# Reordering three stretches of a transformer-layer kernel on eight cores: the last score tiles, the last query store, and the first loads

## The chip, the cores and the metric

The kernel runs on the eight NeuronCores of one Trainium2 chip. Every core runs the same program on its own part of the data, and no core waits for another. The metric is device time in microseconds of the slowest of the eight cores, from the launch to its end.

A core has a matrix engine (TensorE, PE in the rows), a vector engine (DVE), a scalar engine (ACT), GpSimd (POOL) and SyncE (SP). SP and POOL issue the DMA transfers: SP through the hardware queue q1, POOL through the software queue q0. Both feed the same 16 DMA engines. Each of the five engines runs its instructions strictly in the order in which they were written; semaphores alone hold one engine for another.

## The reference

A sandwich layer on x of shape (4, 4096, 1024):

```
x = x + layernorm(attention(layernorm(x)))       # one head of width 1024
x = x + layernorm(ffn(layernorm(x)))             # 1024 -> 4096 -> 1024
attention: q, k, v = split(x W_qkv^T); softmax(q k^T / 32) v W_out^T
ffn: (gelu(x w1 + b1) w2 + b2) * (sum of the two top router weights, renormalised)
```

The reshape in the reference makes each batch row attend over all 4096 of its tokens. A core takes 2048 query tokens and needs the keys of all 4096 tokens of that batch row (its own 2048, tensor `xo`, and the other half's, `xr`).

## The kernel before, in words

The work is folded so that the projections of keys and values vanish. With A = Wq^T Wk / 32 (`am`, built from `wqb` and `wkb`) the scores are q' xn^T, where xn is the normalised input and q' = xn A. With B = Wv^T Wo^T (`bm`) the output of the attention is (P xn) B. All matrix operands are bf16, all sums f32. PSUM has eight banks of 512 columns, used as four pairs.

The stages, in the order in which TensorE runs them, are:

1. **A**: 64 matmuls for the first 512 columns of `am` in eight banks (outer loop over the eight weight chunks c, inner over the eight row tiles i), then 64 for the second half. Between the row tiles 4 to 7 of the second half stand the TensorE transposes of the first four x tiles (`transpose_x`, L316), each of which needs its tile normalised (`stats_x`, `apply_x`; `norm_next` does the statistics of one unit of tiles and applies those of the unit before, `norm_apply` applies only). The weights of chunks 0 and 1 come through SP in f32 into `stage` and are cast by DVE (L225, L227); chunks 2 to 7 come through POOL, cast on the way.
2. **q'**: four groups of 64 matmuls (`project_q`), with the transposes of the other own tiles in between. ACT moves each result to `qst`; SP stores each group's 1 MB to DRAM scratch `qs`.
3. **B**: 128 matmuls (`form_b`). Meanwhile DVE normalises the 16 tiles of `xr`, and SP transposes each by DMA into the key tensor `xnT` (DT, L111). These 16 transposes are in SP's queue in the order of the tiles.
4. **Attention**, 16 query tiles: `scores(i, c)` for c = 0 to 3 (16 matmuls each, 1024 keys; PSUM pair c modulo 2), reduced by DVE (L507) and exponentiated by ACT (L513); `softmax_tail` and `rescale` on DVE; `transpose_p`, a DMA transpose of the 1 MB probabilities by SP; `context(i)` (64 matmuls, pair 2); `copy_u` and `transpose_u` (a 256 KB DMA transpose); `out_proj(i)` (16 matmuls, pair 3); `finish_a` and `finish_b` (the residual and both norms). Tile i+1 is scored ahead of context i. The residual rows `xf` are loaded by POOL (`load_x`), and each of these loads waits for the last q' store, `t_qs[15]`.
5. **FFN**, four groups of 512 tokens: `ffn1` (256 matmuls with `w1b`, gelu on ACT), router, `ffn2` (256 matmuls with `w2b`), `finish_y`. `w1b` (8 MB) lies over `xnT`, so that its eight loads wait for the scores of the last query tile; `w2b` lies over `xn` and waits for the last context. Six ffn1 blocks of the first group stand between `out_proj(13)` and `context(15)`. `load_x2T` is a 1 MB DMA transpose that brings the first group's tokens.

What a wait on a DMA means here: SP and POOL hold a ring of 16 and 24 semaphores, and each DMA also waits for the one a whole ring before it.

The two lines whose waits the prediction speaks of:

```
t_xf[i] = DG(xf[i % 3][:, :], xo[...], [t_x2s.get(i - 3), t_xnb.get(i - 3), t_qs[NQT - 1]])
for n, after in enumerate([None] + [t_x2T[0]] * 3 + [t_pT[NQT - 1]] * 4): load_w1(n, after)
```

Of the kernel before, what the change touches and what calls it, by code (L numbers as in the profile page):

```python
# [13 lines left out]
H = 1024  # L14
# [64 lines left out]
def build_program():  # L79
# [54 lines left out]
    stage = [at(f"stage{c}", H + 512, F32, R1 + (48 + 6 * c) * KB)  # L134
             for c in range(2)]
# [75 lines left out]
    t_mh = V(lambda e: e.memset(mhalf[:, :], -0.5))  # L211

# [7 lines left out]
    for c in range(2):  # L220
        row = slice(c * 128, (c + 1) * 128)
        f, b = stage[c], c * H
        k = DS(f[:, H:H + 512], wk[row, 0:512])
        q = DS(f[:, 0:H], wq[row, :])
        t_k[0].append(V(lambda e, f=f, b=b: e.tensor_copy(  # L225
            wkb[:, b:b + 512], f[:, H:H + 512]), [k]))
        t_q.append([V(lambda e, f=f, b=b, h=h: e.tensor_copy(  # L227
            wqb[:, b + h:b + h + 512], f[:, h:h + 512]), [q])
            for h in (0, 512)])
    t_id = DS(ident[:, :], idb[:, :])  # L230
    t_b1 = DS(b1f[:, :], b1r[:, :])
    for c in range(2, HC):
        row = slice(c * 128, (c + 1) * 128)
        q = DG(wqb[:, c * H:(c + 1) * H], wq[row, :])
        t_q.append([q, q])
        t_k[0].append(DG(wkb[:, c * H:c * H + 512], wk[row, 0:512]))
# [3 lines left out]
    for t in range(NQT):  # L240
        fetch_x(t)
# [101 lines left out]
    for c in range(HC):  # L343
        for i in range(HC):
            tok = am_part(i, 0, c, i, [t_q[c][i // 4], t_k[0][c]])
            if c == HC - 1:
                am_out(i, 0, i, tok)
    norm_next()
    norm_next()
    for c in range(HC):  # L350
        for i in range(4):
            aft = [t_k[1][c]] if i == 0 else []
            if c == 0:
                aft.append(free[i])
            tok = am_part(i, 1, c, i, aft)
            if c == HC - 1:
                am_out(i, 1, i, tok)
    for i in range(4, HC):
        b = i if i < 6 else i - 6
        for c in range(HC):  # L360
            tok = am_part(i, 1, c, b, [free[b]] if c == 0 else ())
        if i == 4:
            norm_next()
            transpose_x(0)
            am_out(i, 1, b, tok)
        elif i == 5:
            norm_next()
            norm_apply()
            am_out(i, 1, b, tok)
            transpose_x(1)  # L370
        elif i == 6:
            am_out(i, 1, b, tok)
            transpose_x(2)
            transpose_x(3)
            norm_next()
        else:
            am_out(i, 1, b, tok)
# [49 lines left out]

    t_bm = []
# [15 lines left out]
    norm_at = {0: (0, 1, 2, 6), 1: (0, 3, 6), 3: (1, 3, 5, 7)}  # L444
    for g in range(NQG):
        toks = []
        for j in range(HC):
            for k in norm_at.get(g, ()):
                if k == j:
                    norm_next()  # L450
            if g == 2 and j == 0:
                norm_apply()
            project_q(g, j, toks)
            for k, at_j in enumerate((1, 3, 5, 6) if g == 0
                                     else (0, 2, 4, 6)):
                if g < 3 and j == at_j:
                    transpose_x(4 * (g + 1) + k)
        d = DS(qs[4 * g:4 * g + 4].rearrange("k p f -> p k f"),
               qst[g % 3][:, :].rearrange("p (k f) -> p k f", k=4), toks)
        for k in range(4):  # L460
            t_qs[4 * g + k] = d
# [9 lines left out]
    t_bmm = Q.now("tensor")  # L471

# [14 lines left out]
    def scores(i, c):  # L487
        p = i % 2
        pr = c % 2
# [3 lines left out]
        if i == 0 and c < 2:  # L493
            aft += [free[2 * pr], free[2 * pr + 1]]
        else:
            aft.append(pair_free[pr])
        for j in range(HC):
# [16 lines left out]
            [mx, t_bmm, t_cf.get(i - 2), t_pT.get(i - 2)])  # L514

# [163 lines left out]
    for i in range(NQT - 1):  # L679
        last = i == NQT - 2  # L680
# [3 lines left out]
        if last:  # L684
            load_x2T(0)
# [3 lines left out]
        if i >= 1 and not last:  # L689
            out_proj(i - 1)  # L690
            finish_a(i - 1)
        scores(i + 1, 3)
        if i + 2 < NQT:
            load_q(i + 2)
        if i >= 1 and not last:
            finish_b(i - 1)
        if i + 2 < NQT:
            load_x(i + 2)
# [40 lines left out]
    def router(g):  # L739
# [18 lines left out]
        a = A(lambda e: e.activation(rex[:, :], rl[:, :], AF.Exp), [a])  # L758
# [221 lines left out]
```

How the kernel before makes its waits and increments, by code:

```python
            def body(e, items=self.items[eng]):  # L65
                seen = {}
                for after, fn, name, inc in items:
                    for s, v in after:
                        if v > seen.get(s, 0):
                            e.wait_ge(sems[s], v)
                            seen[s] = v
                    ins = fn(e)
                    if name is not None:
                        ins.then_inc(sems[name], inc)
```

## Time and profile before

| | us |
|---|---|
| median of three runs of the kernel | 1112.17 (1111.88 and 1136.29 the others) |
| the profiled execution, its own time | 1113.1 |
| its span on the slowest core (core 7) | 1111.6 |
| spans of the eight cores | 1099.0 to 1111.6 |
| TensorE busy in the span | 1069.6 (96%) |
| matmuls | 5120 |

The profile is of one execution. The span runs from the first instruction to the last on one core; the execution's time has 1.5 us more around it. TensorE is busy nearly throughout, so only what leaves it idle, or at the lower of its two clock levels, can be taken away without removing work. The idle is in a few places, listed by the waits of TensorE.

### The profile page before, as it was taken

To read this page: it belongs to the slowest core of one execution; us is meant where nothing else is said; L and a number is where in the kernel's file an instruction comes from. 1 tells how busy PE (TensorE), PEld (TensorE's weight loads), DVE (VectorE), ACT (ScalarE), POOL (GpSimd) and SP (SyncE) were. 2 spreads that over 40 slices of the span, in tenths; PEclk is the share of its full clock that TensorE was granted. 3 is DMA by queue.
4 is the path that set the end of the run, shared out by engine and by line. 5 is a ranking of instruction groups with operands and counts; after the bars stand their busy time and mean duration, and the time that the engine had idled before them with its cause. 6 is when DMAs were issued, how large, how long until landed. Compare 5 with 4: busy or idle time off the path is not lost.

```text
span 1111.6 us, 13934 instructions; the slowest of 8 cores (1099.0 to 1111.6 us)
## 1 busy us (share of the span) xinstructions
PE 1069.6 (96%) x5120; PEld 487.0 (44%) x5120; DVE 347.7 (31%) x715; ACT 313.3 (28%) x511; POOL 95.8 (9%) x167
## 2 busy tenths in 40 slices
PE   5899969999999999999999989999999999999996
PEld 2454424444444444444444434444444444444443
DVE  0663713433333333433333232124003300330033
ACT  0564412332322223332223213302430143013300
POOL 7130000000000000000000141001000000000000
PEclk9999989999999999999999999999999999999998
DMA  9999974134444443234447999993201230121012
GB/s 151 165 181 204 182 135 86 51 92 90 100 104 105 105 94 82 78 79 103 86 105 137 161 138 195 165 194 110 68 1 42 79 69 1 40 79 34 1 39 75
DMA packets 154834, 111.32 MB, mean 100 GB/s; under 512 B 119696, under 2 KB 129680, under 8 KB 154768
## 3 DMA queue, kind: packets, MB, share of 16 engines
q0 software_dynamic: 30544, 62.15, 28.5%
q1 hardware_dynamic: 124224, 48.29, 21.3%
q8 instruction: 41, 0.67, 0.2%
q14 instruction: 25, 0.20, 0.1%
HBM read 88.69 MB, written 25.17 MB: 102 GB/s over the span
## 4 chain that ended last, share of the span: by engine, by line
PE 81%; DMA 9%; DVE 3%; SPq 2%; issue 2%; POOL 1%; ACT 1%; another core or an unknown queue 0%; DVEq 0%; POOLq 0%; ACTq 0%
PE pAll L115 81%; DMA xn<-xr 4%; DMA xn<-xo 2%; DMA pT<-pb 2%; SPq L111 2%; DVE st L274 1%; DVE st L276 1%; POOL wkb L109 1%; DVE xn L291 0%; DVE pb L536 0%; ACT pb L513 0%; DVE nmx L507 0%; POOL wqb L109 0%; DMA xnT<-xn 0%; DVE yt L823 0%
## 5 line engine op out<-in xcount | busy, mean ns | idle before, releaser
L115 PE MATMUL pAll<-xnT,qt 128*128 128x512 bf16 x1024 | 228.0, 381 | 11.4 <-DMA xnT<-xn 8.7
L115 PE MATMUL pAll<-xn,pT 128*128 128x512 bf16 x1024 | 223.6, 379 | 3.0 <-DMA pT<-pb 3.0
L115 PE MATMUL pAll<-x2T,w1b 128*128 128x512 bf16 x1024 | 222.8, 379 | 0.2 <-DVE yt L823 0.2
L115 PEld LDWEIGHTS pAll<-xnT,qt 128*128 128x128 bf16 x1024 | 100.5, 98 | 134.6 <-issue 15.6
L115 PEld LDWEIGHTS pAll<-xn,pT 128*128 128x128 bf16 x1024 | 100.1, 98 | 124.0 <-issue 3.5
L115 PEld LDWEIGHTS pAll<-x2T,w1b 128*128 128x128 bf16 x1024 | 99.7, 98 | 120.4 <-issue 1.5
L507 DVE TENSOR_REDUCE nmx<-pAll 128x1 f32<-128x1024 f32 x64 | 78.1, 1222 | 204.3 <-PE pAll L115 204.3
L513 ACT ACTIVATE pb<-pAll,nmx 128x1024 bf16<-128x1024 f32 x64 | 71.3, 1114 | 184.8 <-DVE nmx L507 184.8
L115 PE MATMUL pAll<-w2b,h1b 128*128 128x512 bf16 x512 | 115.0, 383 | 2.0 <-DMA w2b<-w 2.0
L115 PE MATMUL pAll<-w2b,h1a 128*128 128x512 bf16 x512 | 113.1, 379 | 0.0
L115 PEld LDWEIGHTS pAll<-w2b,h1b 128*128 128x128 bf16 x512 | 50.5, 99 | 63.9 <-issue 4.7
L852 ACT ACTIVATE x2r<-x2r,nm 128x1024 f32<-128x1024 f32 x15 | 17.2, 1148 | 215.1 <-DVE nm L850 215.1
L115 PEld LDWEIGHTS pAll<-w2b,h1a 128*128 128x128 bf16 x512 | 50.1, 98 | 60.4
L823 DVE TENSOR_TENSOR yt<-pAll,b2b 128x1024 f32<-128x1024 f32 (+1 forms) x17 | 19.7, 1161 | 174.0 <-PE pAll L115 174.0
L735 ACT ACTIVATE h1b<-pAll,b1f 128x512 bf16<-128x512 f32 x64 | 43.2, 687 | 60.0 <-PE pAll L115 59.9
L115 PE MATMUL pAll<-bm,uT 128*128 128x512 bf16 x256 | 57.9, 379 | 0.0
L735 ACT ACTIVATE h1a<-pAll,b1f 128x512 bf16<-128x512 f32 x64 | 42.8, 686 | 53.1 <-PE pAll L115 53.1
L115 PE MATMUL pAll<-xnT,am 128*128 128x512 bf16 x256 | 57.4, 379 | 0.0
L565 ACT CAST ub<-pAll 128x1024 bf16<-128x1024 f32 x16 | 16.2, 1012 | 127.1 <-PE pAll L115 127.1
L115 PE MATMUL pAll<-wkb,wqb 128*128 128x512 bf16 x128 | 32.0, 410 | 13.1 <-DVE wqb L227 12.5
L109 POOL DMA_DIRECT2D x2s<-xf x16 | 8.7, 544 | 383.1 <-DVE xf L626 383.1
L115 PEld LDWEIGHTS pAll<-bm,uT 128*128 128x128 bf16 x256 | 25.0, 98 | 30.2
(87 smaller groups left out, 589.0 us busy)
## 6 DMA issues: line engine op xcount, KB each, us to landing
xf<-xo POOLq DMA_DIRECT2D x16, 512.0 KB, 4.4
x2s<-xf POOLq DMA_DIRECT2D x16, 512.0 KB, 3.2
w1b<-w POOLq DMA_DIRECT2D x8, 1024.0 KB, 18.1
w2b<-w POOLq DMA_DIRECT2D x8, 1024.0 KB, 54.0
x2r<-x2s POOLq DMA_DIRECT2D x16, 512.0 KB, 4.5
y<-yt SPq DMA_DIRECT2D x15, 512.0 KB, 2.7
xn<-xo POOLq DMA_DIRECT2D x16, 256.0 KB, 31.1
xn<-xr POOLq DMA_DIRECT2D x16, 256.0 KB, 53.3
```

What stands on the lines that cost most here:

```text
L109: "gpsimd", lambda e, o=o, i=i: e.dma_start(o, i), after)
L111: "sync", lambda e, o=o, i=i: e.dma_start_transpose(o, i), after)
L115: e.matmul(o, l, m, start=f, stop=s), after, sig)
L274: a = V(lambda e, s=s, xt=xt: e.bn_stats(st[:, s:s + 6], xt[:, 0:512]), [t_x[t]])
L276: b = V(lambda e, s=s, xt=xt: e.bn_stats(st[:, s + 6:s + 12], xt[:, 512:1024]))
L507: mx = V(lambda e: e.tensor_reduce(n, pair[pr], AX, ALU.max, negate=True), [tok, t_cf.get(i - 2)])
L513: lambda e: e.activation(o, pair[pr], AF.Exp, bias=n, accum_out=l),
L565: t_ub[i] = A(lambda e: e.copy(o, pair[2]), [t_ctx[i], t_uT.get(i - 2), t_qs[NQT - 1]])
L735: lambda e: e.activation(o, bank[b], AF.Gelu_apprx_tanh, bias=b1f[:, fc:fc + 1]),
L823: a = V(lambda e, c=c: e.tensor_tensor(o[:, c], pair[pr][:, c], b2b[:, c], ALU.add), [t_f2[(t, (c.stop - 1) // 512)], t_b2] + war)
L852: a = A(lambda e: e.activation(x[:, :], x[:, :], AF.Identity, bias=n_), [t_n, t_x2r[t]])
```

## The change

It has four parts, in the order of the program:

1. The first loads. The f32 staging through SP and DVE goes. POOL loads all eight weight chunks with a cast; x tile 0 is fetched after the fourth of the eight second-half `wkb` chunks in place of after the eighth. One small ACT instruction (`t_tab`) stands ahead of everything. TensorE's order around the first four x tiles changes, and a normalisation unit moves from the first stage into the first q' group.
2. The last q' store stands behind all 16 key transposes in SP's queue. The residual loads, which wait for it, go with it.
3. `scores(1, 2)` and `scores(15, 2)` use PSUM pair 3.
4. The last three query tiles: `scores(14)` and `scores(15)` stand back to back, ahead of the contexts 13, 14 and 15. The output projections 12 and 13 follow their neighbouring contexts. The w1 loads hang on other transfers: 1 to 3 on the transposed probabilities of tile 14, 4 to 7 on `uT` of tile 13.

```diff
-    for c in range(2):
...
-        k = DS(f[:, H:H + 512], wk[row, 0:512])
-        q = DS(f[:, 0:H], wq[row, :])
-        t_k[0].append(V(lambda e, f=f, b=b: e.tensor_copy(
-            wkb[:, b:b + 512], f[:, H:H + 512]), [k]))
...
+    t_tab = A(lambda e: e.activation(rex[:, 0:1], eps[:, 0:1], AF.Ln),
+              [t_eps])
-    for c in range(2, HC):
+    for c in range(HC):
         row = slice(c * 128, (c + 1) * 128)
-        q = DG(wqb[:, c * H:(c + 1) * H], wq[row, :])
-        t_q.append([q, q])
+        t_q.append(DG(wqb[:, c * H:(c + 1) * H], wq[row, :]))
         t_k[0].append(DG(wkb[:, c * H:c * H + 512], wk[row, 0:512]))
     for c in range(HC):
         row = slice(c * 128, (c + 1) * 128)
         t_k[1].append(DG(wkb[:, c * H + 512:(c + 1) * H], wk[row, 512:H]))
-    for t in range(NQT):
+        if c == 3:
+            fetch_x(0)
+    for t in range(1, NQT):
         fetch_x(t)
...
-    norm_next()
     norm_next()
...
+    norm_apply()
     for i in range(4, HC):
...
         if i == 4:
+            transpose_x(0)
             norm_next()
-            transpose_x(0)
             am_out(i, 1, b, tok)
         elif i == 5:
+            am_out(i, 1, b, tok)
+            norm_next()
+        elif i == 6:
+            am_out(i, 1, b, tok)
+            transpose_x(1)
+        else:
             norm_next()
             norm_apply()
-            am_out(i, 1, b, tok)
-            transpose_x(1)
-        elif i == 6:
-            am_out(i, 1, b, tok)
             transpose_x(2)
             transpose_x(3)
-            norm_next()
-        else:
             am_out(i, 1, b, tok)
...
-    norm_at = {0: (0, 1, 2, 6), 1: (0, 3, 6), 3: (1, 3, 5, 7)}
+    norm_at = {0: (0, 1, 2, 4, 6), 1: (0, 3, 6), 3: (1, 3, 5, 7)}
...
+        if g < 3:
+            store_q(g, toks)
...
     t_bmm = Q.now("tensor")
+    store_q(3, toks)
...
     def scores(i, c):
         p = i % 2
-        pr = c % 2
+        wide = i in (1, NQT - 1) and c == 2
+        pr = 3 if wide else c % 2
...
-    for n, after in enumerate([None] + [t_x2T[0]] * 3 + [t_pT[NQT - 1]] * 4):
-        load_w1(n, after)
-    copy_u(NQT - 2)
-    transpose_u(NQT - 2)
-    out_proj(NQT - 3)
-    finish_a(NQT - 3)
-    finish_b(NQT - 3)
+    e = NQT - 1
+    copy_u(e - 3)
+    transpose_u(e - 3)
+    load_q(e)
+    for c in range(4):
+        scores(e - 1, c)
+    softmax_tail(e - 1)
+    rescale(e - 1)
+    transpose_p(e - 1)
+    load_x2T(0)
+    for c in range(4):
+        scores(e, c)
+    f_free = {b: t_exp[(e, 3)] for b in range(4)}
+    softmax_tail(e)
+    rescale(e)
+    load_w1(0, None)
+    for n in range(1, 4):
+        load_w1(n, t_pT[e - 1])
+    context(e - 2)
+    copy_u(e - 2)
+    transpose_u(e - 2)
+    transpose_p(e)
+    for n in range(4, 8):
+        load_w1(n, t_uT[e - 2])
+    out_proj(e - 3)
+    finish_a(e - 3)
+    finish_b(e - 3)
+    load_x(e)
+    context(e - 1)
+    copy_u(e - 1)
+    transpose_u(e - 1)
+    out_proj(e - 2)
+    finish_a(e - 2)
+    finish_b(e - 2)
```

How the instructions stand, at the three places that matter. First SP's queue from the third q' store to the first query tiles, before:

```order
L107 DMA qs<-qst2_57 128x4x1024
L111 DMA_TRANSPOSE xnT_43<-xn_47 128x8x128 x6
L107 DMA qs<-qst0_55 128x4x1024
L111 DMA_TRANSPOSE xnT_43<-xn_47 128x8x128 x10
L111 DMA_TRANSPOSE pT0_60<-pb0_58 128x32x128
L107 DMA qt0_71<-qs 128x1024
```

and in the change:

```order
L107 DMA qs<-qst2_55 128x4x1024
L111 DMA_TRANSPOSE xnT_43<-xn_45 128x8x128 x16
L107 DMA qs<-qst0_53 128x4x1024
L111 DMA_TRANSPOSE pT0_58<-pb0_56 128x32x128
L107 DMA qt0_69<-qs 128x1024
```

The last q' store, which stood behind six of the 16 key transposes, stands behind all of them and right ahead of the first probabilities.

Second, TensorE from the scores of tile 14 to the first FFN blocks (`xnT,qt` are scores, `xn,pT` a context, `bm,uT` an output projection, `x2T,w1b` ffn1), before:

```order
L115 MATMUL pAll<-xnT_43,qt0_71 128x512 x48
L115 MATMUL pAll<-bm_54,uT0_69 128x512 x16
L115 MATMUL pAll<-xnT_43,qt0_71 128x512 x16
L115 MATMUL pAll<-xn_47,pT1_61 128x512 x64
L115 MATMUL pAll<-xnT_43,qt1_72 128x512 x64
L115 MATMUL pAll<-xn_47,pT0_60 128x512 x64
L115 MATMUL pAll<-bm_54,uT1_70 128x512 x16
L115 MATMUL pAll<-x2T0_73,w1b_46 128x512 x48
L115 MATMUL pAll<-xn_47,pT1_61 128x512 x64
```

and in the change:

```order
L115 MATMUL pAll<-xnT_43,qt0_69 128x512 x64
L115 MATMUL pAll<-xnT_43,qt1_70 128x512 x64
L115 MATMUL pAll<-xn_45,pT1_59 128x512 x64
L115 MATMUL pAll<-bm_52,uT0_67 128x512 x16
L115 MATMUL pAll<-xn_45,pT0_58 128x512 x64
L115 MATMUL pAll<-bm_52,uT1_68 128x512 x16
L115 MATMUL pAll<-x2T0_71,w1b_44 128x512 x48
L115 MATMUL pAll<-xn_45,pT1_59 128x512 x64
```

The number of matmuls is the same; two whole contexts, two output projections and six FFN blocks now lie between the last scores and context 15, where one context, one projection and the six blocks lay.

Third, SP's queue over the same stretch, before:

```order
L111 DMA_TRANSPOSE pT0_60<-pb0_58 128x32x128
L111 DMA_TRANSPOSE uT1_70<-ub1_68 128x8x128
L111 DMA_TRANSPOSE x2T0_73<-xns 128x8x512
L111 DMA_TRANSPOSE pT1_61<-pb1_59 128x32x128
L111 DMA_TRANSPOSE uT0_69<-ub0_67 128x8x128
```

and in the change:

```order
L111 DMA_TRANSPOSE pT0_58<-pb0_56 128x32x128
L111 DMA_TRANSPOSE x2T0_71<-xns 128x8x512
L111 DMA_TRANSPOSE uT1_68<-ub1_66 128x8x128
L111 DMA_TRANSPOSE pT1_59<-pb1_57 128x32x128
L111 DMA_TRANSPOSE uT0_67<-ub0_65 128x8x128
```

The `uT` of tile 13 (256 KB, needed by output projection 13) now stands behind `x2T` and ahead of the last probabilities.

## Rows read from the trace of the kernel before

**Rows 1.** Spans and mean granted clock of two cores, view of all cores.
```profile
core 5: 1105.6 us, clock 0.992
core 7: 1111.6 us, clock 0.990
```

**Rows 2.** Waits of TensorE on core 7: total, times, longest, in us.
```profile
PE pAll L115 <- DVE wqb L227: 12.5, 2, 9.6
PE pAll L115 <- DMA xnT<-xn: 8.7, 1, 8.7
PE pAll L119 <- DVE xn L291: 2.9, 1, 2.9
```

**Rows 3.** TensorE in order of time, core 7: start, us, count, [idle before, releaser].
```profile
30.61 8.85 PE L115 MATMUL pAll<-wkb,wqb 128*128 128x512 bf16 x40 [0.61 <-ACT am L337]
...
139.92 10.52 PE L115 MATMUL pAll<-xnT,qt 128*128 128x512 bf16 x48 [0.82 <-ACT bm L441]
159.18 12.65 PE L115 MATMUL pAll<-xnT,qt 128*128 128x512 bf16 x48 [8.74 <-DMA xnT<-xn]
173.70 7.07 PE L115 MATMUL pAll<-xnT,qt 128*128 128x512 bf16 x32 [1.87 <-ACT pb L513]
...
643.05 13.97 PE L115 MATMUL pAll<-xn,pT 128*128 128x512 bf16 x64 [2.99 <-DMA pT<-pb]
...
735.85 5.30 PE L115 MATMUL pAll<-w2b,h1b 128*128 128x512 bf16 x16 [2.05 <-DMA w2b<-w]
```

**Rows 4.** The same view on core 5.
```profile
157.82 13.07 PE L115 MATMUL pAll<-xnT,qt 128*128 128x512 bf16 x48 [6.62 <-DMA xnT<-xn]
...
640.96 13.97 PE L115 MATMUL pAll<-xn,pT 128*128 128x512 bf16 x64 [1.84 <-DMA pT<-pb]
```

**Rows 5.** DMA issues of SP in order of time, core 7, key transposes and after.
```profile
132.89 0.39 SPq L107 DMA_DIRECT2D qs<-qst  x1
133.44 23.68 SPq L111 DMA_TRANSPOSE xnT<-xn  x10
171.31 4.99 SPq L111 DMA_TRANSPOSE pT<-pb  x1
```

**Rows 6.** Chain that ended last, core 7: start, us, what; the key transposes.
```profile
141.16 7.20 SPq L111
...
151.73 1.22 SPq L111
...
155.87 3.07 DMA xnT<-xn
```

**Rows 7.** DMA issues of POOL in order of time, core 7.
```profile
138.39 1.58 POOL L109 DMA_DIRECT2D xf<-xo  x3 [72.02 <-DMA qs<-qst]
...
615.97 3.04 POOL L109 DMA_DIRECT2D w1b<-w  x3 [10.45 <-DMA x2T<-xns]
```

**Rows 8.** DMA view, 170 to 173 us: issue, median us to landing.
```profile
pT<-pb SPq DMA_TRANSPOSE x1, 6.7
```

**Rows 9.** DMA issue of SP, core 7, the last probabilities.
```profile
619.42 20.99 SPq L111 DMA_TRANSPOSE pT<-pb  x1
```

**Rows 10.** DMA view, issues in 615 to 620 us: median us to landing.
```profile
pT<-pb SPq DMA_TRANSPOSE x1, 23.5
```

**Rows 11.** DMA view by queue, 625 to 630 us: packets, MB, share of 16 engines.
```profile
q0 software_dynamic: 683, 0.69, 91.2%
q1 hardware_dynamic: 629, 0.16, 35.5%
```

**Rows 12.** The same, 640 to 645 us.
```profile
q1 hardware_dynamic: 3016, 0.76, 78.1%
```

**Rows 13.** The same, 4 to 5 us (q1) and 6 to 7 us (q0).
```profile
q1 hardware_dynamic: 97, 0.19, 93.9%
...
q0 software_dynamic: 16, 0.03, 30.8%
```

**Rows 14.** ScalarE in order of time, core 7, its first work.
```profile
28.58 1.28 ACT L337 ACT_TABLE_LOAD   x1 [28.58 <-PE pAll L115]
```

More of the change, by code:

```diff
@@ L133, in build_program @@
     xnT = at("xnT", HC * TKV, BF16, R1)
-    stage = [at(f"stage{c}", H + 512, F32, R1 + (48 + 6 * c) * KB)
-             for c in range(2)]
     w1b = at("w1b", HC * FF, BF16, R1)
@@ L218, in fetch_x @@
         t_x.append(DG(xn[:, t * H:(t + 1) * H], src[row:row + 128, :]))
-    for c in range(2):
-        row = slice(c * 128, (c + 1) * 128)
-        f, b = stage[c], c * H
-        k = DS(f[:, H:H + 512], wk[row, 0:512])
-        q = DS(f[:, 0:H], wq[row, :])
-        t_k[0].append(V(lambda e, f=f, b=b: e.tensor_copy(
-            wkb[:, b:b + 512], f[:, H:H + 512]), [k]))
-        t_q.append([V(lambda e, f=f, b=b, h=h: e.tensor_copy(
-            wqb[:, b + h:b + h + 512], f[:, h:h + 512]), [q])
-            for h in (0, 512)])
     t_id = DS(ident[:, :], idb[:, :])
     t_b1 = DS(b1f[:, :], b1r[:, :])
-    for c in range(2, HC):
+    for c in range(HC):
         row = slice(c * 128, (c + 1) * 128)
-        q = DG(wqb[:, c * H:(c + 1) * H], wq[row, :])
-        t_q.append([q, q])
+        t_q.append(DG(wqb[:, c * H:(c + 1) * H], wq[row, :]))
         t_k[0].append(DG(wkb[:, c * H:c * H + 512], wk[row, 0:512]))
@@ L344, in build_program @@
         for i in range(HC):
-            tok = am_part(i, 0, c, i, [t_q[c][i // 4], t_k[0][c]])
+            tok = am_part(i, 0, c, i, [t_q[c], t_k[0][c]] if i == 0 else ())
             if c == HC - 1:
                 am_out(i, 0, i, tok)
-    norm_next()
     norm_next()
@@ L426, in project_q, with store_q @@
         toks.append(free[b])
+    def store_q(g, toks):
+        d = DS(qs[4 * g:4 * g + 4].rearrange("k p f -> p k f"),
+               qst[g % 3][:, :].rearrange("p (k f) -> p k f", k=4), toks)
+        for k in range(4):
+            t_qs[4 * g + k] = d
     t_bm = []
@@ L457, in build_program @@
                     transpose_x(4 * (g + 1) + k)
[L458 to L461, printed above, removed]
+        if g < 3:
+            store_q(g, toks)
         if g == 1:
@@ L494, in scores @@
             aft += [free[2 * pr], free[2 * pr + 1]]
+        elif wide:
+            aft += out_free
         else:
@@ L514, in scores @@
             [mx, t_bmm, t_cf.get(i - 2), t_pT.get(i - 2)])
+        if wide:
+            out_free[:] = [t_exp[(i, c)]]
     def softmax_tail(i):
@@ L678, in build_program @@
     transpose_p(0)
-    for i in range(NQT - 1):
-        last = i == NQT - 2
+    for i in range(NQT - 3):
         if i >= 1:
@@ L683, in build_program @@
             transpose_u(i - 1)
-        if last:
-            load_x2T(0)
         scores(i + 1, 0)
@@ L688, in build_program @@
         scores(i + 1, 2)
-        if i >= 1 and not last:
+        if i >= 1:
             out_proj(i - 1)
@@ L692, in build_program @@
         scores(i + 1, 3)
-        if i + 2 < NQT:
-            load_q(i + 2)
-        if i >= 1 and not last:
+        load_q(i + 2)
+        if i >= 1:
             finish_b(i - 1)
-        if i + 2 < NQT:
-            load_x(i + 2)
+        load_x(i + 2)
         softmax_tail(i + 1)
@@ L704, in build_program @@
     t_h1, t_f2, t_y, t_ys, t_x2r, t_s2 = ({} for _ in range(6))
-    f_free = {0: t_exp[(NQT - 1, 2)], 1: t_exp[(NQT - 1, 2)],
-              2: t_exp[(NQT - 1, 3)], 3: t_exp[(NQT - 1, 3)]}
+    f_free = {}
     o_free = {}
@@ L757, in router @@
         f_free[b] = a
-        a = A(lambda e: e.activation(rex[:, :], rl[:, :], AF.Exp), [a])
+        a = A(lambda e: e.activation(rex[:, :], rl[:, :], AF.Exp),
+              [a, t_tab])
         a = V(lambda e: e.tensor_reduce(rsu[:, :], ex, AX, ALU.add), [a])
```

## The prediction

> **What bounds the kernel now.** I read the spans of all cores first, then the page's busy shares, then the waits of TensorE, and then the order of time around each wait. The slowest core is 7, the second slowest 5 [rows 1]. TensorE is busy for 96% of core 7's span and no other engine for more than 31%, so only TensorE's idle time, and its time at the lower clock, can be won back: about 40 us in all. The list of waits is short [rows 2], and the order of time gives each its place [rows 3]: 12.5 us in the first stage for the first weights (9.6 of it before the first matmul), 2.9 us for the first x tile, 8.74 us for the key transposes ahead of `scores(0, 3)`, 1.87 us for an exponential ahead of `scores(1, 2)`, 2.99 us for the probabilities of the last query tile, and 2.05 us for a piece of `w2b`. Nothing waits between 181 and 640 us. The change touches each of these places.
>
> Behind two of the waits TensorE also came back slower. In front of the key wait 48 matmuls took 10.52 us, behind it 12.65 us: the granted clock stood at 1.2 GHz before it returned to 2.4 GHz. That is 2.13 us on core 7; on core 5 it is 13.07 less 10.52, 2.55 us [rows 3, 4]. Behind the w2b wait 16 matmuls took 5.30 us where a third of 48 takes 3.5, so 1.8 us. Behind the waits of 1.87 and 2.99 us the matmuls ran at 2.4 GHz from the start.
>
> **Part 2, the last q' store.** SP issued the store at 132.89 us, ahead of ten of the 16 key transposes, which then took SP 23.68 us [rows 5]. The three residual loads wait for the store and came at 138.39 [rows 7]. While they moved, one transpose held SP for 7.20 us; free of them it takes 1.22 us, and the last landed 3.07 us after its issue [rows 6]. With store and loads behind, the ten need about 1.22 + 0.16 us each, from the end of the sixth at 132: 132 + 13.8 = 145.8 for the last issue to end, landing near 148. TensorE asks for these keys at 159.18 - 8.74 = 150.4. So the wait goes whole, with 2 us to spare: 8.74 + 2.13 = **10.87 us** on core 7, 6.62 + 2.55 = 9.17 on core 5. At the other end, if they moved at the pace of the row (23.68 us for ten) the gain would be nothing. I take the whole, because the long issues stand exactly where the residual loads are in flight. The chain of waits runs through SP's issues here, not through DVE, which has the tiles normalised ahead [rows 6].
>
> Next in line is what the store delays. SP must issue it (0.39 us) before the first probabilities, which came 6 us after the last score of tile 0 (159.18 and 16 slow matmuls, against 171.31); there is room. The residual rows are wanted some 60 us later. The probabilities of tile 0 were issued at 171.31 and landed 6.7 us later, at 178.0 [rows 5, 8]; context 0 began 32 matmuls after 173.70, at 180.6, so 2.6 us were to spare.
>
> **Part 3, pair 3.** `scores(1, 2)` no longer waits for the exponential of `scores(1, 0)`: **1.87 us** [rows 3]. Its spare 2.6 us shrink to 0.7, so the probabilities just make it. What could be late next is `scores(1, 3)`, which needs the exponential of `scores(1, 1)`: that follows the released one by 1.1 us (page, 1114 ns each), so ends near 174.9 on the old axis, and `scores(1, 3)` would start at 173.70 - 1.87 + 3.45 = 175.3. No new wait; both margins under 1 us go into the range.
>
> **Part 4, the last tiles.** `scores(15)` stands one context earlier, and between it and context 15 lie 128 + 32 + 48 matmuls in place of 64 + 16 + 48: 17.3 us more cover for the probabilities. What I must find is whether the DMA queues let them use it. In the profile the last probabilities were issued at 619.42, right behind three w1 loads (615.97), and landed 23.5 us later instead of 6.7 [rows 7 to 10]. The packets say why: in 5 us the software queue moved 683 packets of 1 KB and the hardware queue 629 of 256 B; alone the hardware queue moved 3016 [rows 11, 12]. They take turns by packet, so a 1 MB transpose (4096 packets) drains only when the w1 loads do. Now on core 7's old axis. Context 15 could have begun at 643.05 - 2.99 = 640.1; 336 matmuls at 0.216 us (3.45 per 16) lie between the start of `scores(14)` and it, in either order, so that starts at 567.5 and `scores(15)` at 581.3 instead of 598.5. Tile 14's probabilities (issued some 7 us after its scores, and sharing with w1 load 0) land near 600; `x2T` and w1 loads 1 to 3 start together there; the loads (3 MB at 0.69 MB per 5 us, after 2 us) end near 624, `x2T` at 621. `uT` of tile 13 is behind `x2T` in SP's queue and lands near 625; `out_proj(13)` wants it at 626.1. The last probabilities follow it, and w1 loads 4 to 7 start when `uT` has landed, so the transpose has some 4 us alone (2600 packets) and needs about 11 us for the rest: 637 to 640, wanted at 640. Both meet their user with nothing to spare. I take 2.0 us of new waits; the ends are 0 and, if the probabilities get no head start, 4096 packets at 140 per us, 29 us from 625, so 14 us of wait.
>
> Against that stand 2.99 us on core 7 (1.84 on core 5). The w2b wait goes too: w1 loads 4 to 7 start near 626 instead of behind 619.42 + 23.5 = 642.9, so w2 behind them ends some 17 us earlier, and it was 2.05 late: 2.05 + 1.8 = 3.9 us. Net on core 7: 2.99 + 3.9 - 2.0 = **4.9 us**; on core 5: 1.84 - 2.0 = -0.2. POOL's queue holds the stores of tile 12 behind the w1 loads that wait for `uT`; nobody needs them for 60 us.
>
> **Part 1, the first loads.** The bytes of the first stage are the same and the DMA engines are full from about 5 us on. The software queue's first packets come between 6 and 7 us, though the first issue was at 2.82; the hardware queue was full by 4 to 5 [rows 13]. So without the staged chunks the engines may idle for 0 to 2.1 us; I take 1.5. The last of the eight chunks then lands late by that much, and TensorE, which ended the first half at 30.61 - 0.61 = 30.0, will be paced by the chunks. In exchange the table load (1.28 us on ACT) [rows 14] leaves the gap of 0.61 us at 30.61 [rows 3], x tile 0 comes 1 MB earlier, which covers its 2.9 us wait, and the later tiles' statistics have DVE free. But eight matmuls that covered the last two ACT copies now stand ahead of them, about 1.5 us exposed. Sum: +1.5 - 0.6 - 2.9 + 1.5 and 0.5 for later tiles, **0**; the ends are -2 and +3.
>
> For the table load the Trainium skill ("ScalarE: Activation LUTs", What ACT_TABLE_LOAD costs) gives some 2.66 us for a switch, the drain included. By it the 0.61 would be 2.66, and the sum 2.0 us better, as an estimate from that page. The row shows TensorE waiting 0.61 only, and the measurement decides. The skill's page on DMA ("DMA: Bandwidth & Descriptors", Issuing engine by pattern) speaks against this part: simple loads belong on SyncE, with a first byte 0.4 us sooner. By it the start would lose 0.4 us, not 1.5, an estimate from that page. No row here shows the software queue starting alone.
>
> **The sum.** Core 7: 1111.6 - 10.87 - 1.87 - 4.9 - 0 = 1094.0. Core 5: 1105.6 - 9.17 - 1.87 + 0.2 = 1094.8, now the slowest. With the 1.5 us around the span 1096.3, against the execution's own 1113.1: 16.8 us less. The median of the runs is 1112.17, 0.9 under that execution, which gives **1095.4**, rounded to 1095.
>
> **The rivals.**
>
> *A, as forecast* (0.58): 1091 to 1100.
>
> *B, part of it fails* (0.22): the keys still come late, because store and residual loads were not what held them, or the start costs its 3 us, or the last probabilities wait 5 us more. Each alone gives 1095 + 3 to 5; the store change having no effect at all would give 1095 + 9 to 11, 1106. For it: the rows do not part the store from whatever else was in flight. Against it: the one long issue stands in the residual loads' time, and later ones ran at 1.22. 1100 to 1107.
>
> *C, the start gains* (0.14): the software queue starts at once and x tile 0 was the whole brake, -2 to -3; both new waits of part 4 are zero, -2. 1087 to 1091.
>
> *D, the other side* (0.06): `uT` and the probabilities meet w1 loads 4 to 7 with no head start. `out_proj(13)` waits 3, context 15 waits 14 and restarts at 1.2 GHz (2 us), and with the loads slowed in turn the w2b gain is lost: 19 + 3.9 - 2.0 = 20.9 us above A, near 1116. The kernel is slower than before once the new losses at the end pass 19 us together (1112 less 1095, and the 2.0 counted).
>
> **How the numbers follow.** The time is A's. From 1088 to 1107 the range leaves out part of C and all of D, under 0.2. A difference of 2% (22 us, about what a measurement here can tell from no change) begins below 1089.9 or above 1134.4: faster 0.10, the better part of C and A's tail; slower 0.02, D with more; the rest, 0.88, within.
>
> **What would show it.** Right: no wait on `xnT<-xn` or on `pb L513`, the last ten key transposes done in 15 us or less, the store after them, first context right behind `scores(1, 3)`; `w2b` absent from the waits; the eight spans within 5 us. The step on the last probabilities is wrong if `pT` or `uT` waits exceed 5 us; the step on the start is wrong if matmul 64 ends before 28 or after 33 us. The whole is wrong if a new wait appears between 181 and 595 us, where I left all as it is.

## The result: 0.5% slower, and the profile after

The changed kernel took 1116.2 to 1118.5 us. The ratio to the kernel before is **1.0052, 95% interval [1.0027, 1.0076]**: some 6 us slower, where the prediction had 17 faster, and outside its range. (The median of all four executions, 1158 us, holds two in which one die ran slowed down; this ratio and all below leave such executions out.)

The view of all cores, whose rows of before are [rows 1]: the slowest is core 0, and all eight lie within 4.1 us.

```profile
core 0: 1114.6 us, clock 0.990
...
core 5: 1112.1 us, clock 0.988
...
core 7: 1113.8 us, clock 0.987
```

Core 7 is read below, because the prediction was worked out on it. Its list of TensorE's waits, against [rows 2]: total, times, longest.

```profile
PE pAll L115 <- DMA wkb<-wk: 12.3, 4, 8.5
PE pAll L115 <- DMA pT<-pb: 11.6, 1, 11.6
PE pAll L115 <- DVE xf L628: 8.0, 1, 8.0
...
PE pAll L115 <- DMA xnT<-xn: 0.2, 1, 0.2
```

The wait on the key transposes is gone but for 0.2 us, as forecast, and so is that on the exponential. Two others have come: 11.6 us on the last probabilities, where 2.0 was forecast, and 8.0 us on `xf`, which the prediction doesn't have. TensorE in order of time, core 7, against [rows 3]:

```profile
137.95 10.52 PE L115 MATMUL pAll<-xnT,qt 128*128 128x512 bf16 x48 [0.82 <-ACT bm L439]
148.72 17.43 PE L115 MATMUL pAll<-xnT,qt 128*128 128x512 bf16 x80 [0.24 <-DMA xnT<-xn]
165.98 13.98 PE L115 MATMUL pAll<-xn,pT 128*128 128x512 bf16 x64
...
614.91 10.52 PE L115 MATMUL pAll<-x2T,w1b 128*128 128x512 bf16 x48
637.01 16.12 PE L115 MATMUL pAll<-xn,pT 128*128 128x512 bf16 x64 [11.58 <-DMA pT<-pb]
661.12 5.66 PE L115 MATMUL pAll<-bm,uT 128*128 128x512 bf16 x16 [7.99 <-DVE xf L628]
...
715.76 13.98 PE L115 MATMUL pAll<-w2b,h1a 128*128 128x512 bf16 x64
```

Context 0 starts at 165.98, against 180.6 before: 14.6 us won (12.7 by the two waits, 2.0 because the first scores start at 137.95 and not 139.92). It is still there at 614.91, the first ffn1 block (629.53 before). Then `context(15)` waits 11.58 us and `out_proj(14)` 7.99 us, and at 715.76 `ffn2` starts 6.3 us later than before (709.46). All cores show the same: 10.6 to 14.4 us on `pT`, 1.7 to 8.0 on `xf`, 0 to 3.7 on `uT`.

Behind each of the two waits TensorE comes back slower. The view of stretches, core 7: PEclk is the column behind POOL's, 0.50 being 1.2 GHz.

```profile
637.00:641.00 4.00, 3.99 (x10) 1.49 (x11) 0.00 (x0) 0.00 (x0) 0.00 (x0) 0.50 1.23 161
641.00:645.00 4.00, 4.00 (x20) 1.74 (x18) 0.00 (x0) 0.00 (x0) 0.00 (x0) 0.95 1.27 109
...
661.00:665.00 4.00, 3.88 (x10) 1.40 (x11) 2.62 (x6) 0.00 (x0) 1.14 (x2) 0.50 0.36 144
665.00:669.00 4.00, 4.00 (x20) 1.72 (x19) 1.66 (x4) 0.40 (x1) 3.52 (x5) 0.96 0.38 76
```

So 64 matmuls took 16.12 us in place of 13.98, and 16 took 5.66 in place of 3.62: 4.2 us more.

**Who was late.** First the probabilities. SP's DMA issues on core 7, in order of time, against [rows 5, 9]:

```profile
105.96 38.55 SPq L111 DMA_TRANSPOSE xnT<-xn  x16
145.01 0.39 SPq L107 DMA_DIRECT2D qs<-qst  x1
...
595.64 1.99 SPq L111 DMA_TRANSPOSE uT<-ub  x1
597.98 28.22 SPq L111 DMA_TRANSPOSE pT<-pb  x1
626.40 29.29 SPq L111 DMA_TRANSPOSE uT<-ub  x2
```

The first two lines are part 2 as meant: sixteen key transposes without a gap, the store behind. The last twelve of them were issued from 130 us on and SP was through at 144.5, so the last ten took less than 15 us, as forecast, where they had taken 23.68 [rows 5]. The fourth shows the last probabilities issued at 597.98, 39 us before `context(15)` started with them, and holding SP's sequencer for 28 us. The DMA view gives issue to landing, against [rows 10]; the packets by queue in 605 to 610, in 615 to 620 and in 620 to 625 us stand against [rows 11]:

```profile
pT<-pb SPq DMA_TRANSPOSE x1, 38.9
...
q0 software_dynamic: 777, 0.78, 92.5%
q1 hardware_dynamic: 778, 0.19, 30.6%
...
q1 hardware_dynamic: 788, 0.20, 125.7%
q0 software_dynamic: 150, 0.15, 21.9%
...
q1 hardware_dynamic: 628, 0.16, 97.2%
q0 software_dynamic: 278, 0.28, 50.6%
```

In 605 to 610 us 777 packets of the w1 loads stand to 778 of the transposes: one for one, though a w1 packet carries 1 KB and a transpose's 256 B. From 615 to 625 it is different. The w1 loads 1 to 3 are through (issued at 586.19, 24.9 us to landing), 4 to 7 have just been issued and move only 150 and 278 packets, and yet the transposes move no more than 788 and 628: their own packets now hold the engines four times as long each (125.7% for 788, against 30.6% for 778). From 625 to 635 the two queues move one for one again (634 to 627, 776 to 775).

Then `xf`. POOL in order of time, core 7, and under it VectorE at the same place:

```profile
611.38 3.51 POOL L109 DMA_DIRECT2D w1b<-w  x4 [22.40 <-DMA uT<-ub]
614.84 0.60 POOL L109 DMA_DIRECT2D x2s<-xf  x1
615.39 0.60 POOL L109 DMA_DIRECT2D xns<-xnb  x1
657.26 0.54 POOL L109 DMA_DIRECT2D xf<-xo  x1 [41.27 <-DMA x2s<-xf]
657.81 0.58 POOL L594 TENSOR_TENSOR rs<-ve,mhalf 128x1 f32<-128x1 f32 x1
...
616.90 0.15 DVE L591 TENSOR_SCALAR ve<-mv 128x1 f32<-128x1 f32 x1
658.49 0.16 DVE L612 SCALAR_TENSOR_TENSOR nm<-mv,rs 128x1 f32<-128x1 f32 x1 [41.44 <-POOL rs L594]
658.83 0.75 DVE L622 TENSOR_SCALAR xf<-xf,nm 128x1024 f32<-128x1024 f32 x1 [0.18 <-DVE nm L612]
659.69 1.28 DVE L628 SCALAR_TENSOR_TENSOR xf<-pAll,rs,xf 128x1024 f32<-128x1024 f32 x1
```

Read it from below. `out_proj(14)` needs PSUM pair 3, which the last line frees. That line stands behind `nm`, which waited 41.44 us for a power on 128 numbers that takes POOL 0.58 us. Its input was ready at 617.05. But POOL was standing at `load_x(15)`, which may overwrite its `xf` buffer only when the store `x2s` of tile 12 has landed, and that store had entered the software queue at 614.84, behind four 1 MB w1 loads.

### The profile page after: what moved, and what is told of

It is laid out like the page before. It is cut to its first block, busy times and chain, and to the rows that moved or that the text cites. A ratio compares the mean times of both kernels' runs of the same rounds, so it can differ in the third digit from the quotient of the medians.

```text
span 1114.6 us, 13926 instructions; the slowest of 8 cores (1110.5 to 1114.6 us)
## 1 busy us (share of the span) xinstructions
PE 1070.7 (96%) x5120; PEld 486.9 (44%) x5120; DVE 344.9 (31%) x709; ACT 313.3 (28%) x512; POOL 96.9 (9%) x171
## 4 chain that ended last, share of the span: by engine, by line
PE 77%; DMA 14%; DVE 3%; SPq 2%; issue 2%; POOL 1%; ACT 0%; another core or an unknown queue 0%; DVEq 0%; POOLq 0%; ACTq 0%
PE pAll L115 77%; DMA xn<-xr 4%; DMA x2s<-xf 3%; SPq L111 2%; DMA pT<-pb 2%; DMA wkb<-wk 2%; DMA uT<-ub 2%; DVE st L266 1%; DVE st L268 1%; POOL wkb L109 1%; POOL wqb L109 0%; DMA xnT<-xn 0%; DVE xn L283 0%; DVE pb L538 0%; DVE nmx L507 0%
## 5 line engine op out<-in xcount | busy, mean ns | idle before, releaser
L115 PE MATMUL pAll<-xnT,qt 128*128 128x512 bf16 x1024 | 225.4, 379 | 1.1 <-ACT bm L439 0.8
L115 PE MATMUL pAll<-bm,uT 128*128 128x512 bf16 x256 | 61.2, 394 | 6.9 <-DVE xf L628 4.7
## 6 DMA issues: line engine op xcount, KB each, us to landing
w1b<-w POOLq DMA_DIRECT2D x8, 1024.0 KB, 24.9
```

Of the source, the lines that this page charges most:

```text
L115: e.matmul(o, l, m, start=f, stop=s), after, sig)
```

## The experiments

Ratios are to the kernel before on the same chip, 95% interval behind. They come from three series, in which the kernel before took 1110.5 us (first four rows), 1114.8 (both edits; stores and x first; w1 2 to 7 held; part 2 alone) and 1111.0 (the rest), so differences of some 0.4% between rows of different series are not safe.

| kernel | ratio | TensorE's waits from 560 us on, us (core 7) |
|---|---|---|
| parts 1 to 3, old ending | 0.9905 [0.9891, 0.9919] | w2b 3.6 |
| part 4 alone | 1.0158 [1.0143, 1.0173] | pT 10.5, xf 11.3 |
| change, x of tile 15 later | 1.0007 [0.9997, 1.0018] | pT 11.0 |
| change, w1 4 to 7 held | 1.0097 [1.0083, 1.0112] | xf 17.4, uT 2.8 |
| both edits | 0.9880 [0.9863, 0.9896] | uT 4.6, xf 0.5 |
| both, stores and x first | 0.9881 [0.9861, 0.9900] | uT 3.2 |
| w1 2 to 7 held | 0.9904 [0.9888, 0.9920] | none (core 1: w2b 8.6) |
| w1 in three steps | 0.9924 [0.9879, 0.9970] | none (core 5: pT 3.9, w2b 4.3) |
| part 2 alone | 0.9929 [0.9906, 0.9951] | pT 4.9 |
| part 1 alone | 1.0013 [0.9993, 1.0033] | w2b 2.7 |
| part 3 alone | 0.9974 [0.9953, 0.9995] | none |
| old ending, w1 1 to 3 early | 0.9967 [0.9953, 0.9982] | x2T 11.9 |

### The change without its ending

```diff
-        wide = i in (1, NQT - 1) and c == 2
+        wide = i == 1 and c == 2
...
-    for i in range(NQT - 3):
+    for i in range(NQT - 1):
```

(and the rest of the loop and of the ending as before.)

> The kernel before with parts 1 to 3 of the change (first loads, last q' store, pair 3 in tile 1) and its own ending. If the ending alone takes back the gain (my theory), the time is the one before less about 14 us, 1097 to 1101 us, 0.985 to 0.99 of before, with w2b's wait back. Rival R1, the gain at the store is lost wherever the ending begins, because w1 and the last context's transfers were timed by slack that the later start had given: then 1106 to 1112 us, with a wait on DMA pT or w1b of 5 us or more in the old ending too.

Measured: 1099.9 us, 0.9905. The ending alone takes the gain back; rival R1 falls by its time. One core of eight, 0, does wait 5.0 us on `pT`; the others wait on w2b, 2.1 to 5.1 us in all.

### The ending alone

```diff
+    e = NQT - 1
+    copy_u(e - 3)
...
+    finish_b(e - 2)
```

> The kernel before with the new ending alone (part 4, with pair 3 for scores(15, 2)). The changed kernel shows a wait on DMA pT of 10.6 to 14.4 us before context(15), one on DVE xf of 1.7 to 8.0 us in out_proj(14) and slow matmuls behind them (3 to 5 us), less the w2b wait of 0.4 to 3 us that goes: my theory gives +15 to +20 us, 1127 to 1133 us, 1.013 to 1.018 of before. Rival R2, the ending costs only what the forecast said and the rest was lost in parts 1 to 3: 1112 to 1116 us.

Measured: 1128.3 us, 1.0158, 17.6 us slower; R2 falls. The two halves add up: -1.0% and +1.6% give +0.6%, and the whole change measured +0.5%.

### Tile 15's x behind finish_b(13)

```diff
-    load_x(e)
...
     finish_b(e - 2)
+    load_x(e)
```

> The changed kernel with the load of tile 15's x issued behind finish_b(13) instead of behind finish_b(12). In the changed kernel POOL issues it at 657 us, after 41.3 us idle for a store of x2s, and the power of tile 13's second norm, on POOL right behind it, is what out_proj(14) waits for by way of nm and xf on VectorE. Theory: the wait on DVE xf goes and with it 2 to 8 us; the wait on DMA pT stays at 10 to 14 us; 1109 to 1115 us. Rival R3, POOL's block only hides behind the late transfer: the wait on xf is small but the DMA pT wait grows by as much, or x of tile 15 itself comes late (a wait on DMA xf), and the time stays at 1117.

Measured: 1111.6 us, 1.0007, so about 5 us better than the change (1.0052; by the two intervals 1 to 9). The wait on `xf` is gone on every core, 9.3 to 12.4 us on `pT` stay. TensorE in order of time on the slowest core, 6:

```profile
644.60 15.35 PE L115 MATMUL pAll<-xn,pT 128*128 128x512 bf16 x63 [12.44 <-DMA pT<-pb]
659.79 3.62 PE L115 MATMUL pAll<-bm,uT 128*128 128x512 bf16 x16
```

R3 falls. No DMA and no operation was taken away, only POOL's order changed.

### w1 loads 4 to 7 behind the last probabilities

```diff
     for n in range(4, 8):
-        load_w1(n, t_uT[e - 2])
+        load_w1(n, t_pT[e])
```

> The changed kernel with w1 loads 4 to 7 held until the last probabilities' transpose has landed (they waited on the transpose of u(13)). Theory: that transpose, which took 38.9 us to land beside them, lands within 10 to 15 us of its issue, the wait on DMA pT falls from 10.6 to 14.4 us to 0 to 3 us; the x2s(12) store, which sits in the software queue, lands early too, so POOL's block ends before it matters: 1096 to 1105 us. Rival R4, the first w1 loads and u's own transposes are the load on the engines and the last ones do little: the wait stays above 7 us. Rival R5, w1 itself now comes late: a new wait on DMA w1b of 5 us or more at the first ffn1 and the time at 1105 or above.

Measured: 1121.4 us, 1.0097, where 1096 to 1105 was expected. Half of the theory held. SP, POOL and TensorE in order of time on the slowest core, 2:

```profile
602.35 21.20 SPq L111 DMA_TRANSPOSE pT<-pb  x1
...
626.22 3.50 POOL L109 DMA_DIRECT2D w1b<-w  x4 [32.95 <-DMA pT<-pb]
629.68 0.59 POOL L109 DMA_DIRECT2D x2s<-xf  x1
...
662.38 0.54 POOL L109 DMA_DIRECT2D xf<-xo  x1 [31.55 <-DMA x2s<-xf]
...
632.91 13.98 PE L115 MATMUL pAll<-xn,pT 128*128 128x512 bf16 x64
666.24 5.09 PE L115 MATMUL pAll<-bm,uT 128*128 128x512 bf16 x16 [19.36 <-DVE xf L628]
```

The transpose landed after 23.3 us instead of 43.6 on this core (22.2 instead of 38.9 on core 7), and `context(15)` runs without a wait on all eight. R4 falls, and no wait on w1b came (R5). But my expectation that the store of tile 12 would land early was wrong: the loads held it back on POOL and stood ahead of it in the queue. So POOL's block, which the late probabilities had partly hidden, is seen bare, and it ends later: x is issued at 662.38 us on core 2 and 659.35 on core 7, against 657.26 on core 7 of the changed kernel. TensorE waits 19.4 us on this core, 13.8 to 21.8 on all.

### Both edits

The two diffs above together.

> The changed kernel with both edits together: w1 loads 4 to 7 held until the last probabilities' transpose has landed, and tile 15's x loaded behind finish_b(13). Each edit alone left one wait: the late x load alone left 12.4 us on DMA pT, the held w1 alone left 19.4 us on DVE xf (its POOL stood 31.6 us for the store of x2s(12), which had gone into the queue behind the four held w1 loads). Theory: two separate causes, so together both waits go and about 20 us with them, less 1 to 2 us that the two causes overlapped: 1096 to 1101 us, with 3 to 4 us on DMA uT left. Rival R6, the block only moves on to the next waiter (w2's loads now stand behind the x load on POOL): a w2b wait of 5 us or more and 1104 us or above.

Measured: 0.9880, 13.4 us below its kernel before, with the next one the best ratio here. Against the x edit alone it is 14 us better, against the w1 edit alone 24 (by ratios of two series). TensorE, core 7:

```profile
619.23 5.22 PE L115 MATMUL pAll<-bm,uT 128*128 128x512 bf16 x16 [4.58 <-DMA uT<-ub]
...
634.65 13.98 PE L115 MATMUL pAll<-xn,pT 128*128 128x512 bf16 x64
648.46 3.62 PE L115 MATMUL pAll<-bm,uT 128*128 128x512 bf16 x16
...
675.07 3.61 PE L115 MATMUL pAll<-bm,uT 128*128 128x512 bf16 x16 [0.54 <-DVE xf L628]
```

The wait on `pT` is gone on all cores and that on `xf` but for 0.5 us on this core and 3.7 on core 1, which have moved on to `out_proj(15)`; no w2b wait stands in their place (R6 falls). These two causes account for the whole loss: with both mended the ratio is no worse than with the old ending (0.9905).

### Stores and x ahead of the held loads

```diff
-    for n in range(4, 8):
-        load_w1(n, t_uT[e - 2])
...
     finish_b(e - 3)
     load_x(e)
+    for n in range(4, 8):
+        load_w1(n, t_pT[e])
```

> As the kernel with both edits, but w1 loads 4 to 7 are issued behind finish_b(12) and behind tile 15's x load, so that the stores x2s(12) and xns(12) and that x load enter the software queue ahead of them. Theory: x2s(12) lands within 10 us of its issue at about 605 us, POOL never stands for it, no wait on DMA pT and none on xf; the wait on uT(13), 3 to 4 us beside w1 loads 1 to 3, stays: 1095 to 1100 us, the same as with both edits to 3 us. Rival R7: w1 loads 4 to 7 come too late for the ffn1 units behind context(15), a wait on DMA w1b of 3 us or more.

Measured: 0.9881, the same. The wait on `uT` stayed (6.4 us on core 1, the slowest), and there `x2s` landed after 24.6 us, not within 10, with w1 loads 1 to 3 still ahead of it. POOL stood 20.5 us on that core, with nothing that TensorE needed behind it for so long. The probabilities took 25.1 to 30.8 us to land, against 19.9 to 26.8 with both edits, and core 0 waits 1.0 us for them. No w1b wait (R7 falls).

### w1 loads 2 and 3 held too

The edit is against the kernel before it in this list.

```diff
-    for n in range(1, 4):
+    for n in range(1, 2):
         load_w1(n, t_pT[e - 1])
...
-    for n in range(4, 8):
+    for n in range(2, 8):
         load_w1(n, t_pT[e])
```

> As the kernel before it in this list, with w1 loads 2 and 3 held as well, so that one w1 load alone stands beside the transposes of x2, u(13) and p(15). Theory: the wait on uT(13) of 2 to 4 us and the slow matmuls behind it (5.3 to 5.9 us for 16 of out_proj(13), against 3.6) go too: 3 to 6 us better than with loads 1 to 3 early, 1091 to 1097 us. Rival R8: u(13)'s transpose is late for another reason (it stands behind x2T on SP and lands late alone): the wait stays at 2 us or more and the time is that of the kernel before in this list.

Measured: 0.9904, 1104.9 us against 1101.8 of the kernel before it, where 3 to 6 us less were expected. The first half was right (R8 falls): the transpose landed in 11.6 us on core 7 (8.5 to 17.8 on all), and nothing waits before `ffn2`, which starts at 692.4 to 695.7 on all cores. But w2's loads stand behind w1's in the queue. TensorE on core 1:

```profile
614.27 3.62 PE L115 MATMUL pAll<-bm,uT 128*128 128x512 bf16 x16
...
715.27 3.61 PE L115 MATMUL pAll<-w2b,h1b 128*128 128x512 bf16 x16 [2.44 <-DMA w2b<-w]
...
728.06 4.95 PE L115 MATMUL pAll<-w2b,h1b 128*128 128x512 bf16 x16 [3.66 <-DMA w2b<-w]
```

Some 7 us won at the front are given back there: the waits on w2b come to 8.6 us on this core.

### Three steps

Again against the kernel before it.

```diff
+    for n in range(2, 4):
+        load_w1(n, t_uT[e - 2])
     load_x(e)
-    for n in range(2, 8):
+    for n in range(4, 8):
         load_w1(n, t_pT[e])
```

> The new ending with w1 in three steps: load 1 on the transpose of p(14), loads 2 and 3 on that of u(13), behind the stores of tile 12; x of tile 15; loads 4 to 7 on the transpose of p(15). With loads 2 to 7 held to p(15) all waits before ffn2 went (ffn2 at 694.50 on the core profiled, against 701.76 with loads 1 to 3 early), but w2b, which stands behind w1 in the queue, came 1.9 to 8.6 us late. Theory: loads 2 and 3 start some 7 us earlier, at about 613 us, beside the last third of p(15)'s transpose, which still lands before context(15) needs it at 628: 0.984 to 0.988 of before, w2b waits of 0 to 4 us. Rival R12: w2b's lateness is the total of bytes at the chip's pace, all cores together, not of the start: the waits on w2b stay at up to 8 us and the time at 0.990.

Inconclusive: 0.9924, but the interval reaches from 0.988 to 0.997. In the profiled execution six cores ended between 1088.8 and 1091.9 us, and cores 4 and 5 at 1100.1 and 1104.4, with 1.9 and 3.9 us on `pT` and about 4 on w2b. The last probabilities landed 7.2 to 15.6 us after their issue on four cores and 22.0 to 30.7 on the other four, 4 and 5 among these. R12 is not told apart.

### Each of the other parts alone

Part 2:

```diff
-        d = DS(qs[4 * g:4 * g + 4].rearrange("k p f -> p k f"),
...
+        if g < 3:
+            store_q(g, toks)
...
     t_bmm = Q.now("tensor")
+    store_q(3, toks)
```

> The kernel before with part 2 alone: the last q' store issued behind the 16 key transposes. The forecast priced it at 10.87 us on core 7 and 3.07 to 6.62 us and more on others. All three parts with the old ending measured 0.9905 of before, 10.6 us. Theory: part 2 carries 8 to 10 us of that, 0.991 to 0.993 of before, with the wait of the first scores on the key transposes gone. Rival R9: the first loads (part 1) carry half of it, and part 2 alone gives 4 to 6 us.

Measured: 0.9929, 7.9 us. On core 7 context 0 starts at 170.47 against 180.60, 10.1 us earlier. The end then gives some back: 4.90 us on `pT` against 2.99 [rows 3]. The wait on the keys is gone on six cores, but 1.4 us stay on core 1 and 3.2 on core 0, where context 0 starts at 175.25, no earlier than before (175.22); core 0 is the slowest of this execution. R9 expected 4 to 6 us; the interval is 5.5 to 10.5, and what speaks against its condition is part 1 alone, next.

Part 1: the first loads as in the changed kernel, the rest as before.

> The kernel before with part 1 alone (first loads, x tiles and normalizations reordered, the early Ln). The forecast took 0, between +3 and -2. In the changed kernel the first scores start 2.0 us earlier than before on core 7 (137.95 against 139.92) and 3.3 later on core 4 (140.61 against 137.26), so my theory is 0.997 to 1.003 of before, with the wait on xnT, behind the store, still there. Parts 1 to 3 with the old ending gave 0.9905 and part 2 alone 0.9929; if part 1 carries the difference (rival R10) it reads 0.9975 or less.

Measured: 1.0013; the wait on `xnT` stays (5.1 us on core 7, 11.7 on core 4). R10 falls, and R9 with it.

Part 3, as `wide = i == 1 and c == 2` in the kernel before:

> The kernel before with part 3 alone: the third score tile of tile 1 in pair 3. The wait of 1.87 us on ACT pb goes; whether all of it reaches the end: 0.998 to 0.999 of before, at the edge of what can be told. Rival R11: the context(0) waits for its probabilities instead (core 0 of the changed kernel showed 0.43 us on DMA pT) or the end's transposes give it back: 1.000.

Measured: 0.9974, 2.9 us, of which the interval allows 0.6 to 5.2; the forecast's 1.87 lies in it, and R11 (1.000) falls narrowly. The three parts alone sum to 0.9916, together they measured 0.9905.

### w1 loads 1 to 3 early in the old ending

```diff
-    for n, after in enumerate([None] + [t_x2T[0]] * 3 + [t_pT[NQT - 1]] * 4):
+    for n, after in enumerate([None] + [t_pT[NQT - 2]] * 3 + [t_pT[NQT - 1]] * 4):
```

> Parts 1 to 3 with the old ending, w1 loads 1 to 3 on the transpose of p(14) instead of on that of x2. In the old ending p(15)'s transpose lands 10.5 us after its issue where w1 loads 1 to 3 are issued behind it (core 7, issue 604.6, loads at 605.7) and 26.1 us after it where they are ahead of it (core 0, issue 603.1): the order in which the two enter decides. Theory: loads 1 to 3 now enter some 18 us ahead, at about 588 us, and have mostly left when p(15)'s transpose enters; it lands in 8 to 15 us on every core, no core waits 5 us on it, loads 4 to 7 and w2 start earlier where they were late, and the w2b waits (3.6 to 5.1 us) shrink: 0.986 to 0.990 of before. Rival R13: three loads ahead of the transpose slow it as in the changed kernel (22 to 26 us to land, as with w1 4 to 7 held in the new ending) and x2's transpose and u(12)'s with it: 0.990 to 0.995.

Measured: 0.9967, outside the expected range and R13's, and by the ratios 7 us worse than with the loads where they were. The probabilities did land sooner than behind three loads (issued at 616.93, 15.6 us), and no core waits for them, but they were issued late: `x2T`, which had taken 12 us of SP's time, was now the transpose beside the loads. SP and TensorE on core 7:

```profile
591.06 25.52 SPq L111 DMA_TRANSPOSE x2T<-xns  x1
616.93 13.56 SPq L111 DMA_TRANSPOSE pT<-pb  x1
...
629.09 12.79 PE L115 MATMUL pAll<-x2T,w1b 128*128 128x512 bf16 x48 [11.93 <-DMA x2T<-xns]
```

It landed after 37.9 us. R13 named the price but not the victim.

## Why the prediction was wrong

**Part 2 was right** on the core that it was worked out on: priced at 10.87 us on core 7, it brought the first context forward by 10.1 when alone. On core 0 it brought nothing when alone; in the whole change no core waits over 0.3 us on the keys, and which of the other parts closed that rest is not shown. **Part 3** was right within its interval. **Part 1** was 0 and measured +0.1%, though not by my steps: on core 7 the first half of `am` ends at 29.5 us against 30.0, so the +1.5 for an idle start didn't come. Nor is there a gain: the first matmul starts at 8.4 to 9.6 us on the eight cores before and at 8.4 to 9.7 after, and the first scores at 139.0 on the mean in both. The 2.0 us that core 7 starts earlier are that core's and not the change's; core 4 starts 3.3 later (140.61 against 137.26). By the old ending the three parts give 0.9905, 10.6 us, where the two terms on core 7 had 12.7; the maximum over cores moves less than the slowest core. Core 4 ended last there (1099.4), where it had 1099.0 before: its keys had cost it 3.88 us to begin with, it starts later, and 5.1 us on w2b came.

**Part 4 failed, at "I take 2.0 us of new waits".** Core 7's span closes by the measured terms: 1094.0 forecast, + 9.6 (`pT` 11.6 for 2.0), + 8.0 (`xf`), + 4.2 (1.2 GHz behind both), - 2.0 (the earlier start) = 1113.8, as measured.

*The first of two failed steps is "so the transpose has some 4 us alone (2600 packets)".* The times around it were good: I had `uT` of tile 13 landing at 625 on the old axis, 610.4 on the new, and POOL saw it by 611.4. A gap between loads 1 to 3 and loads 4 to 7 did come, but the transpose couldn't use it. In 610 to 615 us 1155 of its packets moved, and in the ten us after that 788 + 628 = 1416, beside 150 + 278 of the loads, where at the pace of [rows 12], 3016 in 5 us, 2600 take 4.3 us. (And 4 us at that pace are 2400, not 2600.) After 625 the loads took every other turn. The stretch goes with loads 4 to 7: with them held, the transpose moved at the pace that it has alone as soon as loads 1 to 3 were through (core 7, 620 to 625 us: 4184 packets, 117.6%) and landed after 22.2 us. Why its packets take so long beside loads that have only begun is not shown. The bound that I had worked out myself for no head start, 14 us of wait, is near what came (11.6 here, 10.6 to 14.4 on all cores); it came by a slower road than the turn-taking that I had priced, and from an issue 12 us earlier than I had it (597.98, 612.6 on the old axis), so the size is partly luck. With both ends of a range known, I had chosen near the good one on an estimate with "nothing to spare". The landing times on core 7 bear out that it is the company that counts:

| kernel | issued | w1 loads beside it | landed after |
|---|---|---|---|
| tile 0, before [rows 8] | 171.31 | none | 6.7 |
| parts 1 to 3, old ending | 604.65 | 3, issued 1.0 us behind it | 10.5 |
| w1 2 to 7 held | 599.01 | 1 | 11.6 |
| change, w1 4 to 7 held | 602.17 | 3 | 22.2 |
| before [rows 10] | 619.42 | 3, issued 3.5 us ahead | 23.5 |
| stores and x first | 603.86 | 3, and the store `x2s` | 26.1 |
| changed kernel | 597.98 | 7 | 38.9 |

The Trainium skill ("DMA: Bandwidth & Descriptors", Queues, rings and completion order) says that an engine goes round its queues and changes at the packet. The trace agrees where both queues are busy, 777 packets to 778 in 605 to 610 us, at 1 KB and 256 B each. The stretch from 615 to 625 us, 1416 packets to 428, isn't explained by that rule alone.

*The second is "POOL's queue holds the stores of tile 12 [...]; nobody needs them for 60 us".* One instruction did need them: `load_x(15)`, for its buffer, and it stands on POOL itself. I had asked who reads the stored data and not who reuses the buffer, nor what is queued behind that user. The experiment with `load_x(15)` moved, with every operation kept, took some 5 us off; with w1 held the block, itself some us longer, cost 19.4.

**The rivals.** D was the case: its `context(15)` waits 14 and restarts at 1.2 GHz, which is what happened, its time of 1116 was right, and it had 0.06. It was right in size partly by luck: its 3 us on `out_proj(13)` were 0 on core 7 (up to 3.7 on others), the w2b gain that it gave up was kept, and `xf`, which no rival had, came in its stead.

**The new order itself costs nothing, but no gain is shown either.** With the two causes mended it measured 0.9880 against 0.9905 for the old ending. The two stand in different series, though: in microseconds it is 1102.1 against 1099.9, with the kernel before at 1114.8 and 1110.5.

## What to carry to other kernels

When a large load is put beside a DMA transpose, count packets, not bytes, and price the transpose at the whole length of the load, and give it no head start in a gap unless a trace shows it moving there. For each store in a queue ask who reuses its source, on which engine that user stands, and what small operation is queued behind it. If a range has a bad end with a mechanism and a good one with no slack, the bad one deserves most of the chance.

## What the runs showed that I had not expected

- A buffer's reuse can carry a store's lateness onto an engine 41 us idle, and through a 0.58 us operation to TensorE.
- The order of two issues less than 1 us apart goes with some 10 us of landing. With part 1 in the kernel and the old ending (two executions, 16 cores), the last probabilities entered 0.4 to 3.2 us ahead of w1 loads 1 to 3 on twelve cores and landed after 10.5 to 14.7 us; on three cores they entered 0.2 to 0.8 us behind and took 23.9 to 26.1; on one, 0.1 us ahead, 21.1. In the kernel before they are behind on all eight: 20.9 to 24.3.
- Just after w1 loads 4 to 7 were issued, the transposes' own packets took far longer: on core 7 788 packets held 125.7% of the engines' time in 5 us, where 778 held 30.6% in 605 to 610. Cores 0, 4 and 6 show the same in 620 to 625 (770 at 91.2%, 604 at 75.4%, 851 at 84.9%). No run tells the cause apart; it stays open.
- Holding everything back is no cure: with loads 2 to 7 held every earlier wait went, and w2b came up to 8.6 us late.
